# A two-layer transformer: layer 0's ternary weights made in attention group 6, and six of layer 1's differences moved to ScalarE and GpSimd

## The reference

```python
x = L0_attn_x
x = _layernorm(x + _L0_attn_ref(x, L0_attn_w_qkv, L0_attn_w_out, L0_attn_b_out), axis=-1)
x = _layernorm(x + _L0_ffn_ref(x, L0_ffn_W_up, L0_ffn_W_gate, L0_ffn_W_down), axis=-1)
x = _layernorm(x + _L1_attn_ref(x, L1_attn_Wq, L1_attn_Wkv, L1_attn_Wo, L1_attn_bo), axis=-1)
x = _layernorm(x + _L1_ffn_ref(x, L1_ffn_w_gate, L1_ffn_w_up, L1_ffn_w_down), axis=-1)
```

```python
scale = jnp.mean(jnp.abs(w)) + EPS
q = jnp.clip(jnp.round(w / scale), -1.0, 1.0) * scale
```

## Time and profile before

| | before |
|---|---|
| median of 3 runs | 1011.0 us (1010.37 to 1013.32) |
| the profiled execution | 1011.03 us, its span 1009.3 us |
| TensorE busy | 949.5 us, 94% of the span |
| VectorE busy | 693.9 us, 69% |
| ScalarE busy | 589.7 us, 58% |
| GpSimd busy | 347.0 us, 34% |
| layer 0's front, first score to last maximum | 40.95 to 80.10 us |
| layer 1's front, first maximum to last | 435.12 to 484.81 us |

### The profile page before, as it was taken

The page is one execution under the profiler, slowest core; times in us unless marked ns, Lnnn a source line. Parts: engine busy times, 40 slices in busy tenths (PEclk is TensorE's granted clock), DMA queues, the critical chain, the costliest instruction groups (busy, mean ns, idle before and its releaser), DMA issues. The chain is left out here.

```text
span 1009.3 us, 18025 instructions
## 1 busy us (share of the span) xinstructions
PE 949.5 (94%) x6546; PEld 515.2 (51%) x6546; DVE 693.9 (69%) x1535; ACT 589.7 (58%) x1204; POOL 347.0 (34%) x418
## 2 busy tenths in 40 slices
PE   6698999999998999978899999999999998999997
PEld 4352333333354887653334343443434354798896
DVE  2879888888834676677888888888888633433423
ACT  3444777777766335524577777777777768222321
POOL 3031322231123444322337363342625233224332
PEclk9898999999999999998799999999999999999999
DMA  7653211122000200241705062230401000000001
GB/s 245 196 172 107 65 49 43 44 59 64 2 1 19 76 1 8 77 151 48 213 9 176 4 173 72 64 109 28 134 2 40 2 1 1 1 1 22 22 1 42
DMA packets 32996, 64.20 MB, mean 64 GB/s; under 512 B 6095, under 2 KB 22367, under 8 KB 30532
## 3 DMA queue, kind: packets, MB, share of 16 engines
q1 hardware_dynamic: 31564, 58.47, 18.9%
q0 software_dynamic: 1072, 3.80, 1.1%
q10 hardware_dynamic: 272, 0.79, 0.2%
HBM read 50.45 MB, written 12.32 MB: 62 GB/s over the span
## 5 line engine op out<-in xcount | busy, mean ns | idle before, releaser
L1126 ACT ACTIVATE prob<-ps 128x512 f32<-128x512 f32 (+6 forms) x896 | 426.6, 541 | 159.8 <-PE ps L1171 156.7
L1171 PE MATMUL ps<-qop,kop 98*128 98x512 bf16 (+14 forms) x1376 | 271.5, 288 | 1.6 <-ACT prob L1126 0.6
L1157 PE MATMUL ps<-kop,qop 96*128 96x512 bf16 (+3 forms) x896 | 243.8, 357 | 20.9 <-DVE maxes L1056 15.4
L1171 PEld LDWEIGHTS ps<-qop,kop 107*128 107x128 bf16 (+1 forms) x1376 | 113.5, 97 | 212.6 <-ACT prob L1126 118.9
L1200 PE MATMUL ps<-prob,vst 128*32 128x512 f32 (+4 forms) x1792 | 211.2, 543 | 4.7 <-POOL prob L993 2.9
L1056 DVE CUSTOM_DVE_ANT_0 sums<-ps,tri 128x128 bf16<-128x128 f32 (+7 forms) x256 | 180.6, 754 | 20.0 <-PE ps L1157 18.5
L993 POOL TENSOR_TENSOR prob<-prob,keep 128x384 int32<-128x384 int32 (+2 forms) x144 | 121.6, 853 | 191.1 <-ACT prob L1126 190.9
L1056 DVE CUSTOM_DVE_ANT_0 sums<-ps,table 128x960 bf16<-128x960 f32 x128 | 148.0, 1156 | 47.6 <-PE ps L1157 35.4
L1601 PE MATMUL ps<-xs,wffn 128*128 128x512 f32 x640 | 156.2, 397 | 0.9 <-PEq L805 0.9
L1056 DVE CUSTOM_DVE_ANT_0 tri<-ps,table 128x960 bf16<-128x960 f32 x128 | 147.5, 1152 | 1.8 <-PE ps L1157 1.7
L1496 POOL TENSOR_TENSOR hs<-hf,hs 128x512 fp32r<-128x512 f32 x64 | 82.9, 1296 | 151.0 <-ACT hs L1519 142.7
(11 more groups left out here) (103 smaller groups left out, 684.4 us busy)
## 6 DMA issues: line engine op xcount, KB each, us to landing
table<-in_table SPq DMA_DIRECT2D x32, 464.0 KB, 4.7
qop<-q_parts SPq DMA_DIRECT2D x96, 128.0 KB, 2.6
kop<-k_parts SPq DMA_DIRECT2D x48, 128.0 KB, 2.6
kop<-k_parts SPq DMA_DIRECT2D x48, 96.0 KB
q_parts<-qop SPq DMA_DIRECT2D x8, 384.0 KB, 4.0
q_parts<-kop SPq DMA_DIRECT2D x8, 384.0 KB, 2.6
x<-in_x SPq DMA_DIRECT2D x4, 512.0 KB, 5.8
k_parts<-qop SPq DMA_DIRECT2D x4, 384.0 KB, 2.7
```

What stands on the lines that cost most here:

```text
L1126: nc.scalar.activation(prob[0:rows, q % 2, k % HG, lo % CH:lo % CH + hi - lo], ps[0:rows, home["exp", n, k], lo % CH:lo % CH + hi - lo], A ...
L1157: last = nc.tensor.matmul(ps[:, S_BANK + score_slot(L, k)[0] + a // CH, a % CH:a % CH + b - a], qop[0:RD, par, h, i0:i0 + P], kop[0:RD, pa ...
L1171: return nc.tensor.matmul(ps[:, bank, a % CH:a % CH + b - a], lhs, rhs, start=start, stop=True, skip_group_check=True)
```

## The change

- **Layer 0's front.** "abs" moves from batch 0's steps into batch 1's, beside the maxima; "total" and "threshold" move behind the "rows" of group 0. Batch 0's units come in another order, the last "v" of batch 0 goes to the head of batch 1's steps, and the projections rotate over four PSUM banks rather than three (4 to 7; the total now uses bank 6). Values of quad 0 wait until VectorE has read the total. Steps are spread by the width of the maxima, and a "turn" weighs 0.6. x chunks 2 and 3 are loaded right behind chunks 0 and 1, the raw weights only once group 0's operands are there, and units up to 11 are sent ahead of group 1's operand load.
- **Ternary weights.** They are made in group 6, quads 8 to 11, three slices of 128 x 512 behind each quad, twelve in all: the comparison by GpSimd, the step with three operands by VectorE. `below` is a ring of eight slices.
- **Layer 1.** For units 6 to 11 ScalarE copies the whole projection into `rest` behind the first part, and GpSimd subtracts the first part from it in place; VectorE no longer takes part. A bank is free once ScalarE has copied.

```diff
@@ plan_by_table
+        if group == N - 2 and n >= nq - 4:
+            steps += [("ternary", 3 * (n - nq + 4) + k, 0) for k in range(3)]
@@
-PE_SHARE = ({"turn": 1, "unit": 1, "v": 1}, {"turn": 0.85, "unit": 1.72, "v": 1.72})
+PE_SHARE = ({"turn": 0.6, "unit": 1, "v": 1}, {"turn": 0.85, "unit": 1.72, "v": 1.72})
@@ opening_of
-        first = proj.steps(0)
-        for j, step in enumerate((("unit", 2), ("unit", 4), ("v", 2))):
-            first.insert(first.index(step), ("abs", j))
-        at = first.index(("unit", 6))
-        first[at:at] = [("total", 0), ("threshold", 0), ("ternary", 0)]
-        first += [("ternary", 1), ("ternary", 2)]
-        out = [(what, k, 0) for what, k in first]
-
-    width = [hi - lo for _, _, lo, hi in units] if layer.index == 1 else [1] * len(units)
+        out = [(what, k, 0) for what, k in proj.steps(0)]
+
+    width = [hi - lo if layer.index == 1 else hi - lo + 2 * P for _, _, lo, hi in units]
...
-    return out + [("parts", 0, 1), ("rows", 0, 1)] + [("max", k, 2) for k in range(AHEAD[layer.index])]
+    scale = [("total", 0, 0), ("threshold", 0, 0)] if layer.index == 0 else []
+    return out + [("parts", 0, 1), ("rows", 0, 1)] + scale + [("max", k, 2) for k in range(AHEAD[layer.index])]
@@ Projection
-        banks = ((4, 5, 6), (4, 5, 6)) if i == 0 else ((6, 7), (6, 7, 4, 5))
+        banks = ((4, 5, 6, 7), (4, 5, 6, 7)) if i == 0 else ((6, 7), (6, 7, 4, 5))
...
+        if self.i == 0 and b == 0:
+            return [*t, u[0], u[1], f[0], u[2], f[1], u[3], f[2], f[3], v[0], u[4], u[5], f[4], v[1], u[6], f[5], u[7], f[6],
+                    v[2], f[7]]
         if self.i == 0:
...
+            return [("v", TB // 2 - 1), *t, u[0], u[1], f[0], v[0], u[2], f[1], u[3], f[2], v[1], u[4], f[3], ("abs", 0),
+                    u[5], f[4], v[2], ("abs", 1), u[6], f[5], ("abs", 2), u[7], f[6], v[3], f[7]]
...
+    def off_dve(self, u):
+
+        return self.i == 1 and u >= self.half()
@@ act
+            if self.off_dve(k):
+                self.wait_third(act, k - RING)
+                nc.scalar.activation(self.rest[0:r, k % RING, :], src[0:r, :], ACT.Copy,
+                                     scale=0.25 if self.is_q(m) else 1.0).then_inc(self.whole, 1)
@@ pool
+        if what == "unit" and self.off_dve(k):
...
+            nc.gpsimd.tensor_tensor(self.rest[0:r, k % RING, :], self.rest[0:r, k % RING, :],
+                                    self.part[k % RING][0:r, 0, :], ALU.subtract).then_inc(self.rest_behind, 1)
...
+        elif what == "ternary":
+
+            j, cols, home = self.slice_of(k)
+            pool.wait_ge(self.tern, 3 + (k - 7 if k >= 8 else 0))
+            nc.gpsimd.tensor_scalar(self.below[:, home], self.raw[j][:, cols], self.thr[:, 1, j:j + 1], None, ALU.is_lt
+                                    ).then_inc(self.below_set, 1)
@@ dve
-        elif what == "unit":
+        elif what == "unit" and not self.off_dve(k):
...
         elif what == "ternary":
...
+            j, cols, home = self.slice_of(k)
+            dve.wait_ge(self.tern, 3)
+            dve.wait_ge(self.below_set, k + 1)
+            nc.vector.scalar_tensor_tensor(out=K.wffn[:, j, 0, cols], in0=self.raw[j][:, cols],
+                                           scalar=self.thr[:, 0, j:j + 1], in1=self.below[:, home].bitcast(F32),
+                                           op0=ALU.is_gt, op1=ALU.subtract).then_inc(self.tern, 1)
@@ sync
+                for c in range(NC // 2, NC):
+                    sp.dma_start(K.x[:, CT * c:CT * c + CT, :], xv[:, CT * c:CT * c + CT, :]
+                                 ).then_inc(proj.x_loaded[c], 16)
...
-            later = len(proj.units) // 2 + 2 * (1 - i)
+            later = len(proj.units) // 2 + 4 * (1 - i)
@@ gpsimd
+            if i == 0:
+                pool.wait_ge(loaded[0], 16 * operands.loads)
+                for j, wt in enumerate(dram.ffn[0]):
...
@@ tensor
+                        elif k == 0 and i == 0:
+
+                            pe.wait_ge(proj.tern, 1)
```

More of the change, by code:

```diff
@@ L269, in opening_of @@
         due = work * sum(width[:n + 1]) / sum(width[:-2])
-        if layer.index == 0:
-            due = -(-work * (n + 1) // (len(units) - 2))
         while at < len(behind) and given + behind[at][2] <= due + 1e-6:
@@ L337, in __init__ @@
         self.rest1 = sem("rest1_done" + tag)
+        if self.i == 1:
+            self.whole = sem("whole_copied")
+            self.rest_behind = sem("rest_behind")
         self.part2 = sem("part2_done" + tag)
@@ L410, in steps @@
         turns = [("turn", n) for n in range(b * turned, (b + 1) * turned)]
-        if self.i == 0:
-            vs = [("v", v) for v in range(b * 4, b * 4 + 4)]
-            out = [*turns]
-            for j in range(4):
-                for _, u in units[2 * j:2 * j + 2]:
-                    out += [("unit", u), ("finish", u - 1)] if u >= 1 else [("unit", u)]
-                out.append(vs[j])
-            return out if b == 0 else out + [("finish", len(self.units) - 1)]
-        u, t, f = units, turns, [("finish", k) for _, k in units]
+        u, t, f = units, turns, [("finish", k) for _, k in units]
+        v = [("v", k) for k in range(b * TB // 2, (b + 1) * TB // 2)]
+        if self.i == 0 and b == 0:
+            return [*t, u[0], u[1], f[0], u[2], f[1], u[3], f[2], f[3], v[0], u[4], u[5], f[4], v[1], u[6], f[5], u[7], f[6],
+                    v[2], f[7]]
+        if self.i == 0:
+            return [("v", TB // 2 - 1), *t, u[0], u[1], f[0], v[0], u[2], f[1], u[3], f[2], v[1], u[4], f[3], ("abs", 0),
+                    u[5], f[4], v[2], ("abs", 1), u[6], f[5], ("abs", 2), u[7], f[6], v[3], f[7]]
         return [*t[:4], u[0], u[1], f[0], ("weigh", 3), ("decay", 3), u[2], f[1], *t[4:6], f[2], ("divide", 3), ("scale", 3),
@@ L425, in beside_maxima @@
         if self.i == 0:
-            return [*self.steps(1)[:-1], ("finish", len(self.units) - 1, 1)]
+            return self.steps(1)
         first, second = self.steps(1)[:2], self.steps(1)[2:]
@@ L451, in wait_read @@
         else:
-            pe.wait_ge(self.rest1, k + 1)
+            if self.off_dve(k):
+                pe.wait_ge(self.whole, k - self.half() + 1)
+            else:
+                pe.wait_ge(self.rest1, k + 1)
             if self.copies_before(k + 1):
@@ L561, in act @@
                 act.wait_ge(self.abs_sum, k)
[L562 removed]
+            nc.scalar.activation(self.below[:, 0:KD * E], self.raw[k], ACT.Abs, accum_out=self.wsum[:, k:k + 1]
                                  ).then_inc(self.abs_sum, 1)
@@ L567, in second_part @@
         r = self.rows_of(self.units[u][1])
-        act.wait_ge(self.rest1, u + 1)
+        if self.off_dve(u):
+            act.wait_ge(self.rest_behind, u - self.half() + 1)
+        else:
+            act.wait_ge(self.rest1, u + 1)
         self.nc.scalar.copy(self.part[u % RING][0:r, 1, :], self.rest[0:r, u % RING, :]).then_inc(self.part2, 1)
@@ L586, in pool @@
         nc = self.nc
-        if what == "finish" and k >= self.half():
-            self.third_part_behind(pool, k)
+        if what == "unit" and self.off_dve(k):
+            r = self.rows_of(self.units[k][1])
+            pool.wait_ge(self.part1, k + 1)
+            pool.wait_ge(self.whole, k - self.half() + 1)
+            nc.gpsimd.tensor_tensor(self.rest[0:r, k % RING, :], self.rest[0:r, k % RING, :],
+                                    self.part[k % RING][0:r, 0, :], ALU.subtract).then_inc(self.rest_behind, 1)
+        elif what == "finish" and k >= self.half():
+            self.third_part_behind(pool, k)
+        elif what == "ternary":
[3 more added lines that the diff above has]
+                                    ).then_inc(self.below_set, 1)
         elif what == "decay":
@@ L944, in _ @@
                 pool.wait_ge(proj.x_loaded[1], 16)
-                for j, wt in enumerate(dram.ffn[0]):
-                    wt = wt.rearrange("(k p) n -> p k n", p=P)
-                    pool.dma_start(proj.raw[j].rearrange("p (k n) -> p k n", k=wt.shape[1]), wt
-                                   ).then_inc(proj.ffn_loaded, 16)
                 pool.dma_start(K.identb[:], dram.identb).then_inc(K.tri_loaded, 16)
```

34 lines of the change are left out of this document (17 added, 17 removed).

## The result

The changed kernel takes 1014.09 us (median of 22 runs, 1012.93 to 1020.10) beside 1010.91 us of the kernel before (22 runs); ratio 1.0039, 95% interval 1.0027 to 1.0050. It is slower, by 3.2 us between the medians and 3.9 by the ratio; the forecast was 1010 us, 1 us faster and so no change. The time lies in the upper end of the range, which reached to 1015 for a dear comparison. The profiled execution (1016.31 us, 2.2 above the median) has a span of 1014.6 us instead of 1009.3: +5.3.

The account below looks back on a forecast made before the run. TensorE was taken as the bound, dense except at layer 0's front, group 6's end and layer 1's front, where it waits. The terms -7.0 + 10.5 - 4.5 = -1.0 us gave 1010 us from 1011.0, range 999.5 to 1015.

Parts of the forecast that it names:

- the price of the comparison: Group 6: each 128x512 comparison on GpSimd takes 0.6 us, between a copy at 0.609 and the two-input form at 1.155.
- The hold: Group 6: VectorE's steps with two SBUF inputs shut GpSimd out, 0.57 us each, three per quad, less one in the first.
- What follows from the stall: Behind group 6: group 7's first mask +8.4 us, TensorE stalling 1.5 to 3 us apiece, clock at half +1.7.
- The 0.4 that I added for the gather's copy: Group 6's end: VectorE's copy of attention results stands behind its last three-operand step, +0.4 us.
- Rival 2: Group 6: the comparison costs the two-input price, 1.155 us, so twelve add 6.6 us: 1016.6 us, slower; chance 0.12.
- the term for group 6: Group 6's end: comparisons and holds on GpSimd delay masks and stall TensorE, +10.5 us, bounds +8 to +12.
- Rival 1: Group 6: the engines don't shut each other out, or comparisons run in a block and VectorE trails: 1001.8 us; chance 0.28.
- Layer 0's front: -7.0 forecast: Layer 0's front: earlier fourth send and first score, last maximum ending at 73.0 instead of 80.10; bounds -5 and -10.
- The clock term: Layer 0's front: TensorE's clock falls as before, 0 us; full clock would give 2 more.
- Layer 1's front: -4.5 forecast: Layer 1's front: six differences leave VectorE, so maxima run earlier, -4.5 us; bounds -3 and -5.5.
- rival 4: Layer 1's front: differences weren't the bound, TensorE fills the gap: -1 not -4.5, 1013.5 us; chance 0.10 with Rival 3.
- Rival 3: Layer 0's front: raw weights delay sends, gain 2 instead of 7, 1015 us; chance 0.10 together with rival 4.

Follow-up runs that it names:

- v_early_abs: Changed kernel with ternary slices wholly on VectorE (five group 6, seven group 7), moved v back before first scores, ScalarE's third weight pass behind the front: 993.43 us.
- l0_only: The changed kernel with layer 1's differences back on VectorE, so layer 0's part alone: 1019.29 us, ratio 1.0087 to the kernel before.

## Why the prediction was wrong

**What failed is one term: the price of the comparison.** The step was "One input and one output: I take 0.6", next to a copy of the same shape at 0.609. It measured 1.57 with nothing beside it. The upper bound I gave, the two-input form at 1.155, was no bound: the operation with a scalar is dearer than the one with two tensors. With the true price and no hold at all, twelve comparisons add 18.8 us to GpSimd's 7.64 us, of which 5.1 were idle.

**The hold was real and oversized.** I charged 0.57 us three times a quad, from VectorE's and GpSimd's two-input steps; the runs show 0.43 once a quad, the rest falling on VectorE's step (1.10 instead of 0.75), where nobody waited. The two errors partly cancelled: the price was 11.6 us too low over twelve comparisons, the hold 5.0 us too high (eleven of 0.57 instead of three of 0.43); 16.0 us were forecast from mask to mask, 22.19 measured. My forecast 4.14 us a quad was 0.63 + 1.8 + 1.71; it is 0.64 + 4.6 + 0.43, about 5.65.

**What follows from the stall was right in the main.** From mask to mask it was +14.55, and to the first `inv` +16.4. The 1.85 us between are the fallen clock, where I had 1.7: the values of quad 0 and the transposes take 0.87 us more each. The 0.4 that I added for the gather's copy came to nothing: the copy ended at 294.14, and TensorE began the transposes at 294.57 without a wait. TensorE waited for GpSimd, in pieces of 2.7 to 3.9 us instead of 1.5 to 3. Group 7 made up nothing, as said.

**Rival 2 is what happened**, with the sign and the mechanism that I gave it at 0.12 and a larger price. It was said to decide from 0.94 us a comparison, and 1.57 is well beyond. Its time, 1016.6, is close to the profiled execution's own 1016.3, and that is luck: the oversized hold made up for the undersized price. The median, 1014.09, lies inside the range because the range was stretched to take in this rival; the term for group 6, +16.4, is well outside its own bounds of +8 to +12. Rival 1 fell with the price. Neither bound that I had for the operation came from an instruction of its own kind at its width; the only one in the trace, 0.269 us on 4 columns, says nothing of the growth by column.

**Layer 0's front: -7.0 forecast, -6.3 in the profiled execution.** Fourth send 21.3 against 21.89, first score 34.2 against 34.53, last maximum's end 73.0 against 74.05. Where the lost 0.7 us went isn't shown. I had priced the moved v at 1.75, though I let the clock fall, and at half clock it took 3.62. VectorE's waits of 1.73 and 0.85 us behind ScalarE's passes, which I had at 1 in all, look like a cause, but in `v_early_abs` the last of them went and the stretch stayed as long. A reading was off too, without weight in the sum: only two of ScalarE's three passes stood ahead of the fourth send; the third began at 28.58, behind it. The clock term (0 taken, "full clock would give 2 more") is the one that moves: with the clock at 1.00 the stretch from the start of the first score to that of the last maximum is 35.3 us instead of 38.3, and quad 8's mask comes 9.2 to 9.8 us early. My bounds, -5 and -10, held both kinds, but not `l0_only` with its second stretch of low clock, where the mask came 3.3 us early.

**Layer 1's front: -4.5 forecast, -4.8 in the profiled execution, -4.0 alone by the medians.** Its rival 4 fell: the longest wait before a difference is a wait for TensorE now (3.05), and the differences' time is gone.

**Rival 3** (raw weights delay the sends) fell: sends and loads were in time.

## What to carry to other kernels

Before work is moved to an engine, find in the trace that very operation at that width, or measure it: the two neighbours taken as bounds, a copy and an operation on two tensors, both of the same shape, lay both below it, and an error of 1 us came twelve times over. Then put moved work where its engine is idle and where nothing that the next engine waits for stands behind it: twelve comparisons cost 16 us between the masks; with eight of them one stretch earlier and four on VectorE they cost 0.4 us there, and with all twelve slices on VectorE, five before the gather's copy and seven behind, 0.1.
